# Expert results of a two-layer mixture block: scatters from four buffers, read back and stored in pieces

## The reference

```python
# layer 1; layer 0: softmax router, gelu(x @ w1 + b1) @ w2 + b2
logits = xt @ w_gate
top_logits, sel = jax.lax.top_k(logits, TOP_K)          # TOP_K = 2
probs = jax.nn.softmax(top_logits, axis=-1)
h = silu(xt @ w1[e]) * (xt @ w3[e])
y = h @ w2[e]
out[t] = sum over the two chosen experts of probs * y
x = x + out
```

## Time and profile before

| | us |
|---|---|
| three timed runs: median (lowest to highest) | 1110.85 (1109.88 to 1112.46) |
| span of the profiled execution, from its first to its last instruction | 1111.7 |
| TensorE matmul busy in it | 940.4 (85%) |
| VectorE busy | 537.2 (48%) |
| ScalarE busy | 466.6 (42%) |
| GpSimd busy | 339.7 (31%) |

### The profile page before, as it was taken

One profiled execution on the slowest core, in us unless ns is written; L12 is line 12 of the kernel. 1 busy time (PEld: TensorE's weight loads), 2 busy tenths in 40 slices (PEclk: granted clock), 3 DMA queues, 4 the chain that ended last, 5 costly groups with the idle time before them and its releaser, 6 DMA issues. The chain is left out here.

```text
span 1111.7 us, 24268 instructions
## 1 busy us (share of the span) xinstructions
PE 940.4 (85%) x8690; PEld 760.3 (68%) x8690; DVE 537.2 (48%) x1598; ACT 466.6 (42%) x1374; POOL 339.7 (31%) x388
## 2 busy tenths in 40 slices
PE   5899999979787779999986599999986866799990
PEld 3677777744465569999975377777764655699980
DVE  3565656540364511111118698777775665222222
ACT  2677677732233123333324466777764640111100
POOL 2311112000110231111131668888871423211120
PEclk9899999979899589999997899999999776899995
DMA  8211119000000289888832101111000004798953
GB/s 249 74 40 40 40 38 263 2 1 1 0 1 1 87 312 342 324 325 323 304 136 73 39 2 40 40 40 38 0 2 2 2 1 166 283 325 304 314 197 123
DMA packets 48979, 136.03 MB, mean 122 GB/s; under 512 B 15800, under 2 KB 35520, under 8 KB 42880
## 3 DMA queue, kind: packets, MB, share of 16 engines
q1 hardware_dynamic: 45152, 124.67, 32.3%
q0 software_dynamic: 3744, 10.26, 2.4%
HBM read 117.54 MB, written 17.38 MB: 121 GB/s over the span
## 5 line engine op out<-in xcount | busy, mean ns | idle before, releaser
L1058 PE MATMUL lower<-arena 128*128 128x128 f32 x1472 | 176.6, 279 | 18.6 <-ACT arena L1397 6.8
L1058 PEld LDWEIGHTS lower<-arena 128*128 128x128 f32 x1472 | 174.1, 195 | 24.5 <-issue 12.7
L1069 PE MATMUL upper<-arena 128*128 128x256 f32 x552 | 126.6, 379 | 0.0
L2115 POOL DMA_INDIRECT ytok<-arena,dest x46 | 44.1, 959 | 266.7 <-DMA ytok<-arena,dest 129.8
L653 PE MATMUL upper<-wkv,arena 128*128 128x256 f32 x512 | 121.4, 379 | 0.0
L1069 PEld LDWEIGHTS upper<-arena 128*128 128x128 f32 x552 | 101.7, 191 | 12.0
L653 PEld LDWEIGHTS upper<-wkv,arena 128*128 128x128 f32 x512 | 94.0, 190 | 11.2
L1397 ACT ACTIVATE arena<-lower,arena 128x128 f32<-128x128 f32 x184 | 52.5, 369 | 107.7 <-PE lower L1058 107.7
L1906 DVE COPY arena<-upper 128x256 f32<-128x256 f32 x46 | 19.5, 424 | 140.1 <-PE upper L1069 73.1
L689 PE MATMUL upper<-const,arena 128*128 128x128 f32 x512 | 80.4, 280 | 6.4 <-ACT arena L1202 6.2
L624 PE MATMUL upper<-wkv,arena 128*128 128x256 f32 x256 | 72.0, 416 | 10.7 <-ACT arena L1139 6.8
(11 more groups left out here) (247 smaller groups left out, 1755.2 us busy)
## 6 DMA issues: line engine op xcount, KB each, us to landing
arena<-in_ew_dram SPq DMA_DIRECT2D x23, 2048.0 KB
arena<-in_ew_dram SPq DMA_DIRECT2D x23, 1536.0 KB
arena<-in_ctxT_dram SPq DMA_DIRECT2D x16, 1028.0 KB, 5.1
xslot<-zero SPq DMA_DIRECT2D x2, 2967.0 KB, 19.0
arena<-xslot SPq DMA_DIRECT2D x46, 129.0 KB, 4.2
arena<-ytok SPq DMA_DIRECT2D x8, 512.0 KB, 5.9
const<-in_const_dram SPq DMA_DIRECT2D x1, 1156.0 KB, 7.7
x<-in_x_dram SPq DMA_DIRECT2D x1, 1024.0 KB, 5.8
```

Source lines behind the costliest of these rows:

```text
L1058: ins = mm(bank[1 + half][:, i * P:i * P + P], ew[k][:, at:at + P], exT[k % 2][:, c, :], start=(c == 0), stop=(c == KC - 1))
L1069: ins = mm(bank[4 + k % 2][:, 0:D], eh[k % 2][:, i, :], ew[k][:, at:at + D], start=(i == 0), stop=(i == nh - 1))
L2115: G.indirect_dma_start(out=ytok[l], out_offset=bass.IndirectOffsetOnAxis(ap=dest[k][:, 0:1], axis=0), in_=eys[k % 2], in_offset=None).then ...
```

## The change

- Four result buffers `eys[k]` with a semaphore each; the scatter of a tile no longer waits for another one. The wait for a buffer's earlier scatter (now that of tile m-4) moves from `outputs` to `places`.
- Empty slots get destination rows of their own, behind the two lists in a longer `ytok`, different for the four buffers; this takes a new constant C_PAD and two more VectorE instructions per tile.
- Reading back in four pieces of 256 tokens, each a pair of 256 KB transfers with its own semaphore, into `xn` and `outT` instead of a tile of its own.
- In layer 1 each token tile's last add signals by itself, and SP stores x in four pieces of 256 KB.
- To make room among the semaphores, three of the self attention's (`wow`, `bow`, `wfw`) become one, and the load of `normw` counts on the semaphore of its neighbours, so that two waits for these loads include it.

```diff
+PIECES = 4
-C_PLACE = C_TOKEN + NT
+C_PAD = C_TOKEN + NT
+C_PLACE = C_PAD + EB
+    c[:, C_PAD:C_PAD + EB] = TOPK * (TOK + 1) + p[:, None] + P * np.arange(EB)[None]
...
-        eys = [ar.take(D) for _ in range(2)]
-        eyg = ar.take(NT, TOPK, D)
-        xrow = eyg.rearrange("p t i d -> p (t i d)")[:, 0:NT * ROW].rearrange("p (t w) -> p t w", w=ROW)
+        eys = [ar.take(D) for _ in range(EB)]
+        xrow = ar.take(NT, ROW)
+        eyg = [xn[:, :, :], outT[:, :, :].rearrange("p c n -> p (c n)").rearrange("p (t d) -> p t d", t=NT)]
...
             def expert_results(l):
-                for k in range(2):
-                    sp.wait_ge(ms[f"ys{k}"], 16 * (l + 1) * ((NTILE + 1 - k) // 2))
-                for h in range(2):
+                for k in range(EB):
+                    sp.wait_ge(ms[f"ys{k}"], 16 * (l + 1) * OF[k])
+                for h in range(PIECES):
                     for i in range(TOPK):
-                        first = i * (TOK + 1) + 1 + h * TOK // 2
+                        first = i * (TOK + 1) + 1 + h * TOK // PIECES
...
             expert_results(1)
-            sp.wait_ge(x_ready, 6)
-            sp.dma_start(out.rearrange("(t p) d -> p t d", p=P), x[:, :, :]).then_inc(out_stored, 16)
-            sp.wait_ge(out_stored, 16)
+            for h in range(PIECES):
+                mine = slice(h * NT // PIECES, (h + 1) * NT // PIECES)
+                sp.wait_ge(x_ready, 5 + mine.stop)
+                sp.dma_start(out.rearrange("(t p) d -> p t d", p=P)[:, mine, :], x[:, mine, :]).then_inc(out_stored, 16)
+            sp.wait_ge(out_stored, 16 * PIECES)
...
                 def outputs(m, k, it):
-                    after(dve, q[f"ys{k % 2}"], 16 * (l * (OF[k % 2] + OF[k % 2 + 2]) + EB // 2 * it + k // 2))
                     dve.wait_ge(q["dnw"], base + m + 1)
-                    V.tensor_copy(eys[k % 2], bank[4 + k % 2][:, 0:D]).then_inc(q["dnc"], 1)
+                    V.tensor_copy(eys[k], bank[4 + k % 2][:, 0:D]).then_inc(q["dnc"], 1)
 
                 def places(m, k, it):
...
                     after(dve, q["dest"], base + m)
+                    after(dve, q[f"ys{k}"], 16 * (l * OF[k] + it))
+                    V.scalar_tensor_tensor(unfilled[:, :], exs[k][:, D:D + 1], 0.0, const[:, C_PAD + k:C_PAD + k + 1],
+                                           ALU.is_equal, ALU.mult)
                     V.tensor_tensor(unlike[:, :], exs[k][:, D + 1:D + 2], tilef[:, bass.ds(m, 1)], ALU.not_equal).then_inc(q["unlike"], 1)
-                    dve.wait_ge(q["unlike"], base + m + 1)
-                    V.scalar_tensor_tensor(dest[k][:, :], unlike[:, :], float(TOK + 1), exs[k][:, D:D + 1], ALU.mult, ALU.add)\
-                     .then_inc(q["dest"], 1)
+                    dve.wait_ge(q["unlike"], 2 * (base + m) + 1)
+                    V.scalar_tensor_tensor(based[:, :], unlike[:, :], float(TOK + 1), exs[k][:, D:D + 1], ALU.mult, ALU.add)\
+                     .then_inc(q["unlike"], 1)
+                    dve.wait_ge(q["unlike"], 2 * (base + m) + 2)
+                    V.tensor_tensor(dest[k][:, :], based[:, :], unfilled[:, :], ALU.add).then_inc(q["dest"], 1)
...
-                    dve.wait_ge(gathered[t // (NT // 2)], 16 * TOPK * (l + 1))
+                    dve.wait_ge(gathered[t * PIECES // NT], 16 * TOPK * (l + 1))
...
                     pool.wait_ge(q["dest"], base + m + 1)
-                    if m:
-                        pool.wait_ge(q[f"ys{(m - 1) % 2}"], 16 * (l * ((NTILE + m % 2) // 2) + (m - 1) // 2 + 1))
                     pool.wait_ge(q["dnc"], base + m + 1)
                     G.indirect_dma_start(out=ytok[l], out_offset=bass.IndirectOffsetOnAxis(ap=dest[k][:, 0:1], axis=0),
-                                         in_=eys[k % 2], in_offset=None).then_inc(q[f"ys{k % 2}"], 16)
+                                         in_=eys[k], in_offset=None).then_inc(q[f"ys{k}"], 16)
```

More of the change, by code:

```diff
@@ L203, in perceiver_block @@
         wa_loaded = sem("wa_loaded")
-        normw_loaded = sem("normw_loaded")
         x_ready = sem("x_ready")
@@ L215, in perceiver_block @@
         blank = sem("blank")
-        gathered = [sem(f"gathered{h}") for h in range(2)]
+        gathered = [sem(f"gathered{h}") for h in range(PIECES)]
         blanked = sem("blanked")
@@ L363, in perceiver_block @@
         exT = [exT2[:, k, :, :] for k in range(2)]
-        eys = [ar.take(D) for _ in range(2)]
-        eyg = ar.take(NT, TOPK, D)
-        xrow = eyg.rearrange("p t i d -> p (t i d)")[:, 0:NT * ROW].rearrange("p (t w) -> p t w", w=ROW)
+        eys = [ar.take(D) for _ in range(EB)]
+        xrow = ar.take(NT, ROW)
+        eyg = [xn[:, :, :], outT[:, :, :].rearrange("p c n -> p (c n)").rearrange("p (t d) -> p t d", t=NT)]
         zero = sb("zero", [P, ROW])
         unlike = sb("unlike", [P, 1])
+        unfilled = sb("unfilled", [P, 1])
+        based = sb("based", [P, 1])
         dest = [sb(f"dest{k}", [P, 1], U32) for k in range(EB)]
@@ L383, in perceiver_block @@
         xslot = [nc.dram_tensor(f"xslot{l}", [NTILE * P, ROW], F32, kind="Internal").ap() for l in range(2)]
-        ytok = [nc.dram_tensor(f"ytok{l}", [TOPK * (TOK + 1), D], F32, kind="Internal").ap() for l in range(2)]
+        ytok = [nc.dram_tensor(f"ytok{l}", [(TOPK + 1) * (TOK + 1) + EB * P, D], F32, kind="Internal").ap() for l in range(2)]
         rw0 = sb("rw0", [P, KC, E_])
@@ L433, in cross_loads @@
                     cross_weights(1)
-                    sp.dma_start(normw[:, :, :], io["normw"]).then_inc(normw_loaded, 16)
+                    sp.dma_start(normw[:, :, :], io["normw"]).then_inc(wa_loaded, 16)
                 if l == 1:
@@ L480, in expert_results @@
             def expert_results(l):
-                for k in range(2):
-                    sp.wait_ge(ms[f"ys{k}"], 16 * (l + 1) * ((NTILE + 1 - k) // 2))
-                for h in range(2):
+                for k in range(EB):
+                    sp.wait_ge(ms[f"ys{k}"], 16 * (l + 1) * OF[k])
+                for h in range(PIECES):
                     for i in range(TOPK):
-                        first = i * (TOK + 1) + 1 + h * TOK // 2
-                        sp.dma_start(eyg[:, h * NT // 2:h * NT // 2 + NT // 2, i, :],
-                                     ytok[l][first:first + TOK // 2, :].rearrange("(t p) d -> p t d", p=P)).then_inc(gathered[h], 16)
+                        first = i * (TOK + 1) + 1 + h * TOK // PIECES
+                        sp.dma_start(eyg[i][:, h * NT // PIECES:(h + 1) * NT // PIECES, :],
+                                     ytok[l][first:first + TOK // PIECES, :].rearrange("(t p) d -> p t d", p=P))\
+                          .then_inc(gathered[h], 16)
             cross_loads(0)
@@ L805, in fold_output @@
                 q = selfs[0]
-                pe.wait_ge(wa_loaded, 48)
+                pe.wait_ge(wa_loaded, 64)
                 pe.wait_ge(x_ready, 1)
@@ L810, in fold_output @@
                         ins = nc.tensor.transpose(bank[4][:, o * D + i * P:o * D + i * P + P], wout[:, i, o * P:o * P + P], ident)
-                ins.then_inc(q["wow"], 1)
+                ins.then_inc(q["foldw"], 1)
                 for o in range(KC):
@@ L814, in fold_output @@
                              const[:, C_CS + o * 2 * D:C_CS + o * 2 * D + D], start=(o == 0), stop=(o == KC - 1))
-                ins.then_inc(q["bow"], 1)
+                ins.then_inc(q["foldw"], 1)
                 pe.wait_ge(q["wfc"], 1)
@@ L820, in fold_output @@
                                  const[:, C_CS + o * 2 * D:C_CS + (o + 1) * 2 * D], start=(o == 0), stop=(o == KC - 1))
-                    ins.then_inc(q["wfw"], 1)
+                    ins.then_inc(q["foldw"], 1)
             def self_short():
@@ L1267, in fold_output @@
                 q = selfs[0]
-                act.wait_ge(q["wow"], 1)
+                act.wait_ge(q["foldw"], 1)
                 A(woT.rearrange("p c d -> p (c d)"), bank[4][:, :], copy).then_inc(q["wfc"], 1)
                 for i in range(KC):
-                    act.wait_ge(q["wfw"], i + 1)
+                    act.wait_ge(q["foldw"], i + 3)
                     A(wf[:, i, :], bank[5 + i][:, :], copy).then_inc(q["wfc"], 1)
@@ L1729, in added @@
                         stats(n)
-                dve.wait_ge(q["bow"], 1)
+                dve.wait_ge(q["foldw"], 2)
                 dve.wait_ge(ln_norm, 2 * NT)
@@ L1938, in experts @@
                             dve.wait_ge(q["cwbc"], NT)
-                        ins = V.scalar_tensor_tensor(x[:, t, :], eyg[:, t, i, :], gsm[:, 2 + i, t:t + 1], x[:, t, :],
+                        ins = V.scalar_tensor_tensor(x[:, t, :], eyg[i][:, t, :], gsm[:, 2 + i, t:t + 1], x[:, t, :],
                                                      ALU.mult, ALU.add)
-                        if t < NT - 1 or i == 0:
+                        if i == 0 or (l == 0 and t < NT - 1):
                             mine(ins)
-                    if t < NT - 1 and l == 0:
```

(9 more changed lines are left out.)

## The result

The changed kernel takes 1092.34 us in the median of four runs (1090.45 to 1093.16), beside 1110.37 us for the kernel before on the same chip: a ratio of 0.9834, 95% interval 0.9815 to 0.9854, or 18.4 us less. The forecast was 15.3 us less, 1095.6 us with a range of 1091.5 to 1102.0.

The account below looks back on a forecast made before the run. TensorE was taken to bound layer 0's loop, scatter waits layer 1's later loop, and serial scatters, read-back, adds and store the end. Gains 4.5 + 5.4 + 2 x 1.7 + 2.0 = 15.3 us gave 1095.6 us, range 1091.5 to 1102.

Parts of the forecast that it names:

- Loop of layer 0: Layer 0's tile loop: TensorE is busy throughout, so removing the scatter waits gains nothing.
- Loop of layer 1: Layer 1's tile loop: without scatter waits its last 14 tiles keep 5.52 us each, gain 4.5 us, bounds 0 and 4.5.
- 0.3 us to spare: Layer 1's loop: added VectorE steps, under 0.4 us a tile, hide in 0.67 us of idle before the copy.
- The last scatters: End of layer 1: last landing 4.4 us after TensorE's end instead of 9.8, gain 5.4 us.
- the same 3.11: End of layer 1: the last scatter's landing was taken to stay at 3.11 us.
- Read-back: Both layers, four pairs: adds start 4.1 us after the first issue instead of 5.8, gain 1.7 us each, bounds 0 and 3.5.
- The last scatter of layer 0: End of layer 0's loop: it could go up to 2.9 us earlier; gain taken as 0, bounds 0 and 2.9.
- Store: End of the kernel, four pieces: last landing 2.4 us instead of 4.4, gain 2.0 us, bounds 0 and 2.6.
- DMA engines as the bound: Rival, layer 1's loop: DMA engines set the pace, so 4.5 us are missing, 1100.1 us; chance 0.13.
- Scatters one behind the other: Rival, scatter queue: it takes one at a time, so only read-back and store gain, 5.4 us, 1105.4 us; chance 0.06.
- Transfers paid in series: Rival, read-back: each 256 KB transfer begins only when the one before landed, a loss, 1148 us; chance 0.05.
- The gap: Rival, VectorE: a 12.8 us standstill at the loop's start could move into the steady loop, 1108.4 us; chance 0.06.

Follow-up runs that it names:

- e11: The kernel before, unchanged, run once more for a second trace: 1113.84 us.
- e5: The changed kernel, unaltered, timed once more as the level to compare with and for a second trace: 1092.61 us, ratio 0.9852 to the kernel before.
- e9: The kernel before with the two further VectorE instructions a tile, but one shared unread row for all empty slots: 1109.68 us, ratio 0.9996.
- e6: The kernel before with rows of their own for empty slots and two further VectorE instructions a tile; two buffers and all waits kept: 1104.88 us, ratio 0.9963.
- e4: The changed kernel with only two result buffers, GpSimd still waiting for no scatter: 1093.03 us, ratio 0.9857 to the kernel before.
- e10: The changed kernel with one row per buffer for the empty slots, four rows in all: 1093.28 us, ratio 0.9835 to the kernel before.
- e2: The changed kernel, but x stored by one 1 MB transfer after the last add: 1092.95 us, ratio 0.9856 to the kernel before.
- e3: The changed kernel with its four buffers, but GpSimd again waits before each scatter until the one before has landed: 1099.80 us, ratio 0.9929.
- e1: The changed kernel, but results read back in two halves, a pair of 512 KB transfers each: 1096.31 us, ratio 0.9888 to the kernel before.

## Why the prediction was right, point by point

**Loop of layer 0: nothing.** Held: 191.6 and 191.0 us from the first token scatter to the last matmul, against 190.0 and 191.5.

**Loop of layer 1: 4.5 us.** The mechanism held: TensorE waits for no scatter and keeps 5.52 to 5.55 us a tile. The size was somewhat high. The table has 3.3, but its stage takes in the first tile, and that was shorter in the first trace of the kernel before, where the gap came just ahead of it (1.9 us from the first output matmul to the next tile's hidden matmuls, in the other three traces 3.1 to 3.4). The 20 tiles after it, before and changed, in the columns of the earlier trace rows:

```profile
960.70:1075.59 114.89, 111.94 (x841) 105.45 (x839) 32.22 (x99) 11.94 (x20) 17.95 (x19) 1.00 0.87 305
954.93:1065.91 110.98, 110.98 (x841) 106.52 (x840) 38.05 (x140) 11.94 (x20) 19.17 (x20) 1.00 0.91 323
```

The second traces have 114.3 (e11) and 110.4 us (e5), which makes 3.9 us in the mean. How long the loop with the old waits takes differs by execution: TensorE waited 2.9 us for VectorE in the first, 2.1 in e11, and the 20 tiles of e9, which has these waits and two more instructions a tile, took 117.4 us. The cover was as worked out: "0.3 us to spare" is now the 0.33 us of idle before the copy at 1066.11.

**The last scatters: 5.4 us.** Measured 5.8. What failed is the value of one term, "the same 3.11" for the last landing: it is now 2.5 us (1074.32 to the read-back's issue at 1076.86), because the empty tiles no longer write all 128 rows to one place. In the part by part I gave the rows of their own no price at all, gain or loss: they stood among what had to be there for the rest. e6 and e9 show that they are worth some 4 us in the kernel before, of which 3.5 are found at the ends of the two layers. Inside the loop the reason that I gave, the waits taken away, is sufficient (e4: two buffers, no wait on GpSimd, full gain). Whether the rows alone would also speed the loop stays open: three traces with one shared row have VectorE wait 61.5 to 69 us there, the one with rows of their own 17.5, but that one is of a fast execution, and the median landings in layer 1 (5.0, 4.6 and 5.2 us against 4.7) do not separate them. The two parts overlap: once the scatters wait for nobody, the rows bring only 0.7 us and 0.9 us (e10).

**Read-back: 1.7 us a layer.** The start came 2.3 and 2.6 us sooner, more than the halfway value (3.4 us from issue to first add, not 4.1). In layer 1 that passes on, with the adds a little tighter. In layer 0 it does not all pass on: the adds took 1.7 us more. With the earlier issue, TensorE's next matmuls come 1.5 to 2.0 us sooner after the last output matmul (19.5 us, before 21.0 and 21.5), so the path by way of the adds was read rightly. Against my 1.7 the net was 2.6 in layer 1 and 0.9 in layer 0. The sign of trouble that I had named, adds waiting for a second piece, did show, at 0.64 us once.

**The last scatter of layer 0: 0.** It was 0.9 us, of which e10 lays all on the rows (8.1 against 7.2 us).

**Store: 2.0 us.** Measured 2.3; e2 shows the cause.

**Sum:** 15.3 forecast, 15.8 by stages, 16.4 and 18.4 by the two timings. The rest of the first timing's 18.4 lies in stretches that scatter between executions; no run here assigns it. That the sum comes so close is in part luck: the loop gave 0.6 us less than forecast (1.2 by the table), while the last scatters, the last scatter of layer 0 and the store gave 0.4, 0.9 and 0.3 us more, the first two for a reason that the forecast did not have, the rows of their own.

**The rivals.** DMA engines as the bound: no, the loop ran at a share of 0.86 without a gap in TensorE. Scatters one behind the other: no, in layer 1 of the changed trace they leave some 5.5 us apart and those that the trace dates land 7.1 us after their issue in the median; e3 shows what one at a time costs. Transfers paid in series: no. The eight transfers of the read-back in layer 1 take (the line's own view, from 1070 us)

```profile
DMA to landing us min/median/max: 2.7/4.6/5.6
```

and all have landed 9.1 us after the first issue, where eight in series at 4.6 us would need 37. By the Trainium skill (DMA: Bandwidth & Descriptors, Bandwidth) transfers are best batched to 1 MiB and more, which is about throughput, and here e1, with 512 KB, starts its adds 1.9 to 2.1 us later than the 256 KB do. The gap: it is not the program's (e11).

## What to carry to other kernels

Look at the addresses of padding, not only at its bytes: 128 rows sent to one dummy row made a scatter land 0.7 us later, and where each transfer waits for the one before, every such delay at the end is paid in full (four of them here). Cut a transfer where the start of the work waits for its first part or the end for its last, and count in the issue time of the pieces (0.4 to 0.5 us each here). And compare stages over more than one trace before reading a stall as the kernel's: a gap of 12.8 us in the trace before was one execution's.

## What I had not expected

Rows of their own as a gain, above. The second is in layer 0: moving the adds 4 us earlier put them beside GpSimd's five subtractions (578.11 to 583.51), and there an add took 1.16 us, after it 0.48. In e1 they start at 582.63, and only the first one is long:

```profile
578.35 5.04 POOL L2023 TENSOR_TENSOR arena<-arena 128x512 f32<-128x512 f32 x5
...
582.63 1.05 DVE L1954 SCALAR_TENSOR_TENSOR x<-xn,gsm,x 128x256 f32<-128x256 f32 x1 [6.77 <-DMA outT<-ytok]
583.71 0.48 DVE L1954 SCALAR_TENSOR_TENSOR x<-outT,gsm,x 128x256 f32<-128x256 f32 x1
```

In the kernel before, the adds began at 584.29, after GpSimd was done (583.94). That it does not take the new place of the results read back is shown by e6, which keeps the old one: its first add begins under the last subtraction, and the first two adds take 1.28 us together, where two take 1.00:

```profile
575.78 5.04 POOL L2016 TENSOR_TENSOR arena<-arena 128x512 f32<-128x512 f32 x5
580.34 1.28 DVE L1947 SCALAR_TENSOR_TENSOR x<-arena,gsm,x 128x256 f32<-128x256 f32 x2 [7.05 <-DMA arena<-ytok]
```

The five subtractions take 5.40 us beside the adds, 5.04 without. The Trainium skill says that GpSimd shares a read and a write interface with VectorE and conflicts with its instructions that have two inputs in SBUF (Advanced Engine Details and Errata, GPSIMD Details); the adds have two such inputs, and the traces agree, with 1.16 us beside GpSimd and 0.48 after it. No run moved GpSimd's work away, so the cause is argued from the overlap in these traces and not shown. Third, with several scatters under way each one lands later, 7.2 us in the median over both layers against 5.8, and it costs nothing, since nobody in the loop waits for it.
